# A decoder layer with experts on one core: result biases loaded into the self-attention's weights, padding written expert by expert, the main tiles' first row behind the early ones, opening loads in two steps, epsilon added by ScalarE

## The reference, cut to what matters

```python
x = layernorm(x + attn(x, x, x, sa_..., causal=True), ln1_g, ln1_b)
x = layernorm(x + attn(x, ctx, ctx, ca_..., causal=False), ln2_g, ln2_b)   # ctx: 4 x 1024 rows
# experts: 8 of them, each 256 -> 1024 -> 256; a row goes to its two best
topw, topi = top_k(softmax(xf @ router_w + router_b), 2); topw = softmax(topw)
h  = gelu(xf @ e_w1[e] + e_b1[e]);  eo = h @ e_w2[e] + e_b2[e]
x = layernorm(x + sum_e combine[:, e] * eo[e], ln3_g, ln3_b)
```

## Time and profile before

| | us |
|---|---|
| median of 3 executions | 1027.35 (1026.60 to 1029.22) |
| profiled execution, its own time | 1027.64 |
| span in the profile, first to last instruction | 1025.9 |
| TensorE busy | 969.8 (95%) |
| VectorE, ScalarE, GpSimd busy | 561.4, 583.2, 350.7 |

### The profile page before, as it was taken

How to read it: one execution, slowest core, us unless ns; L and a number is a source line. 1 busy time by engine, 2 the same in 40 slices (tenths; PEclk the granted TensorE clock), 3 DMA queues, 4 the chain that set the end, 5 groups by cost and what they waited for, 6 DMA issues and landing times.

```text
span 1025.9 us, 18784 instructions
## 1 busy us (share of the span) xinstructions
PE 969.8 (95%) x6052; PEld 578.2 (56%) x6053; DVE 561.4 (55%) x964; ACT 583.2 (57%) x1200; POOL 350.7 (34%) x469
## 2 busy tenths in 40 slices
PE   5999999999999999999999999984978999999995
PEld 3545544343445543435443354234977999999974
DVE  3746587877766777777778777622221121121216
ACT  2464556777765677775677657881322444343442
POOL 8465952343144443314554150112140111111114
PEclk9999999999999999999999999997988999999998
DMA  7533452003024011204333030012021243224116
GB/s 220 142 109 100 107 133 82 23 21 105 1 65 122 23 42 41 55 1 120 131 119 97 11 93 1 32 53 72 16 98 36 103 138 128 94 68 169 48 53 209
DMA packets 72001, 84.22 MB, mean 82 GB/s; under 512 B 10753, under 2 KB 65537, under 8 KB 71809
## 3 DMA queue, kind: packets, MB, share of 16 engines
q1 hardware_dynamic: 66432, 66.06, 22.2%
q0 software_dynamic: 5504, 17.34, 5.0%
HBM read 38.89 MB, written 12.63 MB: 50 GB/s over the span
## 4 chain that ended last, share of the span: by engine, by line
PE 86%; DMA 5%; DVE 2%; issue 1%; POOL 1%; SPq 1%; another core or an unknown queue 1%; ACT 1%; DVEq 0%; ACTq 0%; POOLq 0%
PE o_bank L867 15%; PE a_bank L850 15%; PE v_slot L1315 12%; PE v_slot L822 11%; PE a_bank L1307 9%; PE a_bank L790 6%; PE a_bank L805 4%; PE v_slot L826 3%; PE o_bank L1307 3%; PE v_slot L889 2%; DMA inputs<-slots_in 2%; PE v_slot L875 1%; PE v_slot L827 1%; PE a_bank L770 1%; DMA w_ca_wv<-in_ca_wv 1%
## 5 line engine op out<-in xcount | busy, mean ns | idle before, releaser
L1041 DVE TENSOR_REDUCE max_q<-v_slot 128x1 f32<-128x1024 f32 (+3 forms) x352 | 399.7, 1172 | 103.4 <-PE v_slot L822 65.7
L981 ACT ACTIVATE probs<-a_bank 128x512 f32<-128x512 f32 (+1 forms) x688 | 363.7, 589 | 111.6 <-PE a_bank L850 103.5
L1321 ACT ACTIVATE hidden<-a_bank,b 128x128 f32<-128x128 f32 x216 | 79.0, 367 | 171.2 <-PE a_bank L1307 149.1
L850 PE MATMUL a_bank<-q_stack_cross,k_stack_cross 99*128 99x512 bf16 x512 | 163.3, 381 | 0.7 <-ACT probs L981 0.5
L822 PE MATMUL v_slot<-k_stack_cross,q_stack_cross 96*128 96x512 bf16 x512 | 147.3, 379 | 0.0
L1315 PE MATMUL v_slot<-stack_or_weights,hidden 128*128 128x256 f32 x576 | 132.0, 383 | 14.0 <-DVEq L1157 13.9
L867 PE MATMUL o_bank<-probs,v_cross 128*32 128x512 f32 x1024 | 132.2, 603 | 0.1
L1315 PEld LDWEIGHTS v_slot<-stack_or_weights,hidden 128*128 128x128 f32 x576 | 107.7, 192 | 27.9 <-DVEq L1157 14.1
L1307 PE MATMUL a_bank<-x_col,stack_or_weights 128*128 128x128 f32 x864 | 113.0, 282 | 7.0 <-ACT hidden L1321 5.2
L1307 PEld LDWEIGHTS a_bank<-x_col,stack_or_weights 128*128 128x128 f32 x864 | 108.9, 198 | 9.6 <-ACT hidden L1321 5.4
L850 PEld LDWEIGHTS a_bank<-q_stack_cross,k_stack_cross 99*128 99x128 bf16 x512 | 44.3, 97 | 109.3 <-ACT probs L981 70.3
(11 more groups left out here) (209 smaller groups left out, 1142.5 us busy)
## 6 DMA issues: line engine op xcount, KB each, us to landing
stack_or_weights<-parts SPq DMA_DIRECT2D x96, 128.0 KB, 2.4
k_stack_cross<-parts SPq DMA_DIRECT2D x96, 128.0 KB, 2.4
stack_or_weights<-in_e_w SPq DMA_DIRECT2D x12, 1024.0 KB
q_stack_cross<-parts SPq DMA_DIRECT2D x48, 128.0 KB, 2.4
inputs<-in_ctxT POOLq DMA_DIRECT2D x4, 1024.0 KB, 6.6
stack_or_weights<-in_e_w SPq DMA_DIRECT2D x8, 512.0 KB
y_got<-token_out SPq DMA_DIRECT2D x16, 256.0 KB, 6.3
x_slots<-slots_in SPq DMA_DIRECT2D x30, 129.0 KB
```

The source lines that it names most:

```text
L850: last = nc.tensor.matmul(bank[:, i * cols:(i + 1) * cols], lhs, q_stack[kind][0:KM, G * u + j, q0:S], start=True, stop=True)
L981: nc.scalar.activation(probs[tile % PB][:, js[0]:js[-1] + 1, q0:S], a_bank[at % AS][:, 0:len(js) * (S - q0)].rearrange("p (j t) -> p j t", ...
L1041: nc.vector.tensor_reduce(most, rows, X, ALU.max, negate=True).then_inc(v_free, 1)
L1321: nc.scalar.activation(hidden[:, f, :], h_bank[f % HB][:, 0:P], ACT.Gelu, bias=b1[:, bass.ds(e * FC + f, 1)]).then_inc(flow.gelu_done, 1)
```

## The change

1. **Opening.** SyncE issues `sa_wq` and `sa_wk`, waits for `xT`, and then issues `ca_wv`, `ca_wk`, `sa_wv` and four bias columns. ScalarE itself issues the two bias columns it waits for. GpSimd loads `ctxT` after the constants and after `xT` has landed, and `x` behind its part of split 2. The memset of `k_stack_cross` goes; SyncE copies those rows from the other stack by two DMAs.
2. **Result biases.** The four weights of self-attention lie in one tile, and `b2` is that tile. SyncE loads it behind norm_turn of the last batch's self-attention.
3. **Last scatters.** "rank" issues four of the eight; the other four stand behind the result of the second expert's first tile. VectorE counts the tiles before it finishes that tile.
4. **Padding.** SyncE writes the padding of experts 0 and 1, and in the loop that of expert 2p+i+2 between its weights and its rows, and waits for it.
5. **Handover.** The two loads behind the early tiles' rows now bring main tile 0's rows, so that the last early tile transposes them; VectorE passes them on by increments, and TensorE's own transposition goes.
6. **End.** VectorE no longer adds epsilon; ScalarE does, into `fin_rstd`, and waits for it stand on ScalarE and GpSimd.

The diff, cut to its core:

```diff
@@ in_order
-    order = [("load_x", 0), ("load_ctx", 0), ("load_res", 0), ("constants",), ("more_constants",)]
+    order = [("load_x", 0), ("constants",), ("load_ctx", 0), ("more_constants",)]
...
-    for step, behind in ((("weights",), ...
+    for step, behind in ((("load_res", 0), ("split", 0, 2)), (("result_biases",), ("norm_turn", B - 1, 0)), (("weights",), ...
@@ decoder_layer
+        self_weights = sb("self_weights", [P, 4 * DC, D])
+        b2 = self_weights
...
-        b2 = sb("b2", [P, E, D])
@@ attention_sync
-                for n in ("sa_bq", "sa_bk"):
-                    sp.dma_start(bias[n][:, :], ...).then_inc(bias_in, 16)
+            sp.wait_ge(xt_in, 16)
+            for n in ("ca_wv", "ca_wk"):
+                sp.dma_start(w[n][:, :, :], ...).then_inc(cross_in, 16)
             sp.dma_start(w["sa_wv"][:, :, :], ...).then_inc(wv_in, 16)
-            for n in ("ca_wk", "ca_wv"):
...
+                elif k == "result_biases":
+                    sp.wait_ge(v_free, NO.v["out", B - 1, 0] + 1)
+                    sp.dma_start(b2[:, :, :], ...).then_inc(moe_const, 16)
...
             for e in range(EARLY):
-                end = expert_tiles(sp, early, e, lambda g, i: load_tile(sp, early, g, e * CAP + i * P))
-            for k in range(2):
-                load_tile(sp, early, ...end + k..., 0)
-            sp.wait_ge(v_free, NO.v["o_turn", len(UNIT_LIST) - 1] + 1)
-            sp.dma_start(b2[:, :, :], ...).then_inc(moe_const, 16)
+                expert_tiles(sp, early, e, lambda g, i: load_tile(sp, early, g, e * CAP + i * P))
@@ attention_gpsimd
                 elif k == "load_ctx":
+                    else:
+                        pool.wait_ge(xt_in, 16)
...
-                elif k == "more_constants":
-                    nc.gpsimd.memset(ones_rows(k_stack[1]), ONE_PAIR).then_inc(const_made, 1)
...
-                    early_part(pool, ev[1], lambda g: store_tile(early, g))
+                    if ev[1] < 2:
+                        early_part(pool, ev[1], lambda g: store_tile(early, g))
+                    else:
+                        store_tile(early, first_of_second(pool))
+                        scatter_late(2)
+                        scatter_late(3)
+                        early_part(pool, 3, lambda g: store_tile(early, g))
@@ attention_vector
-                        finish_tile(dve, early, 1, first_of_second(dve))
+                        second = first_of_second(dve)
+                        copy_column(dve, early, second + 1)
                         count_tiles(dve)
+                        keep_results(dve, early, 1, second)
+                        copy_row(dve, early, second + 2)
@@ block.sync
-            for e in range(E):
-                end = sp.value_load(end_i[0:1, e:e + 1], ...)
-                sp.dma_start(slots_dram[bass.ds(end, P), :], pad_rows).then_inc(pads_out, 16)
-            sp.wait_ge(pads_out, 16 * E)
+            for e in range(2):
+                pad_all(e)
+            sp.wait_ge(pads_out, 32)
             sp.wait_ge(scattered_late, 16 * 2 * QT)
             sp.wait_ge(counts_ready, 1)
...
+            for k in range(2):
+                first = sp.value_load(from_i[0:1, 0:1], ...)
+                load_tile(sp, early, ...early_count(sp) + k..., first)
...
                     load_weights(sp, 2 * pair + i + 2, i)
+                    pad_all(2 * pair + i + 2)
+                    sp.wait_ge(pads_out, pair * 32 + 16 * (i + 3))
+                    sp.sem_inc(passed, 1)
                     load_all(2 * pair + i + 2)
@@ block.tensor
-            transpose_row(pe, main, 0)
@@ block.scalar
+            for n in range(TT // FT):
+                sc.wait_ge(var_ready, FT * (n + 1))
+                nc.scalar.activation(fin_rstd[:, cols], fin_mv[:, cols, 1], ACT.Identity, bias=eps[:, :]).then_inc(fin_eps, 1)
+                if n and n - 1 not in ON_VECTOR:
+                    scale_back(n - 1)
@@ block.vector
+            dve.wait_ge(early.xcol_ready, count + 1)
+            dve.sem_inc(main.row_ready, 1)
+            dve.sem_inc(main.t_full, 1)
+            dve.sem_inc(main.xcol_ready, 1)
             dve.wait_ge(early.row_ready, count + 2)
-            copy_row(dve, main, 0)
-            copy_column(dve, main, 0)
             copy_row(dve, main, 1)
...
-                nc.vector.tensor_scalar(fin_rstd[:, cols], fin_mv[:, cols, 1], EPS, None, ALU.add).then_inc(var_ready, 1)
```

63 lines of the change are left out of this document (40 added, 23 removed).

## The result

| | changed kernel | kernel before, timed beside it |
|---|---|---|
| median of 5 runs | 1023.23 us (1020.91 to 1024.27) | 1028.97 us (1026.60 to 1033.53) |
| ratio | 0.9946, 95% interval 0.9929 to 0.9964 | |
| profiled execution | 1023.70 us, span 1022.0, granted clock 0.982 | 1027.64 us, span 1025.9, granted clock 0.982 |

What follows compares the result with a forecast made beforehand. TensorE, busy 95% of the span, was taken as the bound, with time to gain at its waits, lower clock and both ends. Terms -1.4 - 11.3 - 0.9 - 4.0 - 2.0 + 6.3 - 0.2 = -13.5 gave 1013.9 us, range 1006.5 to 1019.5.

Steps and rivals of the forecast that it cites:

- Opening: From the start to the first maxima: they begin 1.4 us earlier, bounds 0 and -2.2.
- The step on `xT`: In the opening: `xT` lands at 6.8 us instead of 8.1, sharing the DMA engines with two weights only.
- that on `ctxT`: In the opening: `ctxT`, issued at about 6.9 us, takes 7.0 and lands at 13.9 against 14.5.
- Result biases: First result near 698 us: the wait for the biases' load goes, -11.3 us; the earlier load costs 0, at most +1.
- -0.9 of clock: Behind the first result's wait: the lower clock may come or not, so half of 1.7 us was taken.
- Scatters and padding: Stop at 754 us: four scatters at a time instead of eight shorten it, -4.0 us, bounds -7.1 and +5.
- Handover: Early to main tiles near 781 us: -2.0 us, of it -1.3 start and -0.7 clock; bounds 0 and -4.7.
- The sum's third of a clock loss: Behind the handover: a third of the 2.3 us lost to the lower clock is regained, -0.7 us.
- Padding in the loop: At expert 2: padding behind two weights delays its rows, one TensorE stop, +6.3 us, bounds 0 and +10.
- The rival by which the padding passes the weights: At expert 2: padding lands 2 us after issue, the +6.3 are gone, 1007.6 us; chance 13%.
- the prediction's reckoning from that figure: At expert 2: by the skill page's 2 us, padding is back at about 814.3 and the term is 0.
- End: Last pairs: VectorE loses a 0.33 us step but GpSimd's pace stays, -0.2 us, bounds -0.8 and +0.5.

Runs made afterwards that it cites:

- e4: Changed kernel with the padding of experts 2 to 7 written in one go behind expert 1's rows, none in the loop; 1010.8 us, ratio 0.9905.
- e5: The changed kernel as it is, timed again in another group; 1017.1 us, ratio 0.9954.
- e14: Changed kernel with only the result biases' load moved from before six stack copies to behind the row maxima; 1014.5 us, ratio 0.9949.
- e3: Changed kernel with the whole opening of the kernel before; 1012.0 us, ratio 0.9913.
- e6: Changed kernel with both the opening of the kernel before (e3) and the padding ahead of the loop (e4); 1007.5 us, ratio 0.9875.
- e13: Changed kernel with the residual's rows loaded behind the first maxima's parts and the second stack's ones written by VectorE; 1010.9 us, ratio 0.9903.
- e11: e9 with the residual's rows loaded behind the second split again, as in the changed kernel; 1006.6 us, ratio 0.9856.
- e9: e7 with the new opening, residual behind the first maxima's parts, ones by VectorE, no waits for `xT`; 1000.9 us, ratio 0.9801.
- e15: e10 with the second stack's ones copied by SyncE again, as in the changed kernel; 1005.5 us, ratio 0.9837.
- e7: e6 with the result biases' load moved from before six stack copies to behind the row maxima; 1003.1 us, ratio 0.9821.
- e8: e3 with the result biases loaded after the last batch's row loads again, as in the kernel before; 1019.0 us, ratio 0.9975.
- e12: e7 with the last batch's eight scatters in one place again; 1002.2 us, ratio 0.9824.
- e16: e10 with the old handover, VectorE's two copies and TensorE's transposition, again; 1007.7 us, ratio 0.9862.
- e18: e10 with epsilon added by VectorE again, as in the kernel before; 1002.1 us, ratio 0.9766, in another group than e10.
- e10: e9 with context and cross weights waiting until `xT` has landed, as in the changed kernel; 1001.5 us, ratio 0.9804.
- e1: Changed kernel with the residual's rows loaded behind the first maxima's parts; 1015.7 us, ratio 0.9939.

## Why the prediction was wrong, step by step

- **Opening, forecast -1.4, was +5.0 to +8.5** in the four profiles with exactly this opening (the changed kernel, e4, e5, e14); the medians put what it loses against the old one at 3 to 5 us (e3, e6 against e4, e13). The failing step reads: "`x` is issued between two splits where GpSimd has idle time." It looked at GpSimd and not at the DMA engines, whose busy share in the trace of before was 0.76 from 10 to 20 us and 0.74 from 20 to 25. e11 prices it at 5.8 us on top of e9. The second is a cost that the sum never had: SyncE's two copies of ones, counted neither in issue time (1.41 us) nor in the queue of the row maxima (e15: 1.5 us in its profile, at most 4 by its time). The step on `xT` held (7.12 for 6.8), that on `ctxT` in this profile (14.39 for 13.9), but the load took 6.2 to 10.8 us in the twelve profiles with the gate, which no bound of mine had. "Everything behind is a chain of TensorE and VectorE work, so it shifts as a whole" held: the lag is 8.5 us from 80 to 520.
- **Result biases, -11.3 with -0.9 of clock, were -14.3 at their place**, as the first result's wait and the lower clock both went. But this was wrong: "the six copies behind it on SyncE's queue share the DMA engines with it for about as long, which covers them if TensorE needs them no sooner; I cost it at 0, at most +1." TensorE needed them sooner: the stop is 1.48 to 2.80 us in the eight profiles with the load there, and e7 shows 4.4 us with the clock. The net of the term was 6.3 us (e8 against e3).
- **Scatters and padding, -4.0, were -3.7 in the profile after** and -7.7 in that of e5. The first is within the bounds, the second 0.6 past them. The reason was wrong: I costed the scatters by their number. e12 shows that eight in a row cost nothing with two paddings beside them. In the profile after a stop of 2.19 us remains, in e5 none.
- **Handover, -2.0, was -4.7 and -3.1** (e5); e16 has 3.8. TensorE idles 2.0 us (forecast 3.5) in all 18 profiles with the new handover. Behind it the clock stays up in nine of them, the changed kernel's among them, and falls in the other nine, e5's to 0.59 from 774 to 778 us; that is the 1.6 us between the two values. What decides it is open. The sum's third of a clock loss was a mean of two cases, and in this profile it was luck.
- **Padding in the loop, +6.3, was +7.0.** The mechanism, its place and its size held: landing at 810.25 after 7.51 us, rows at 814.8, one stop at expert 2, none later. The rival by which the padding passes the weights fell. The Trainium skill, "DMA: Bandwidth & Descriptors", "Anatomy of one DMA", gives its fixed cost of about 2 us for a DMA on GpSimd's path and counts nothing that stands ahead of it. This write, on SyncE's queue behind two loads of 1 MB each, took 7.51 us, so the prediction's reckoning from that figure, 814.3, does not hold here. A load with nothing ahead of it does take 2.16 us.
- **End, -0.2.** The row "rest and end" is -1.5, and every one of the 18 experiments has -0.5 to -1.8 there, e18 with VectorE's epsilon too (-1.0). So epsilon is not what makes it; the rest may be the one profile of before.

The misses of the rows are +9.9, +4.9, -2.1, +0.3, -2.7, +0.7 and -1.3, 9.6 us in the profile; by the medians the miss is 7.8 us. Two of the failed steps are of one kind, a load moved into a stretch whose DMA traffic was not read; the third, the copies of ones, was not counted at all.

What would have shown the miss in time was the view of the DMA issues over the stretch into which a load is moved, with what is due there.

The experiments point past both kernels: e9 and e10 (new opening with the residual behind the first maxima and the ones by VectorE, padding ahead of the loop, biases in the calm stretch, new handover) run at 1000.9 and 1001.5 us, 0.980 of the kernel before, 19 to 20 us faster in the same group. The gate and the split scatters can go.

## What to carry to other kernels

A load that is moved off a path lands on another one: before moving it, read what is in flight and what is due in the 6 us behind its new place, on all DMA engines and on the issuing engine's queue, and not only whether the issuer is idle. When several small waits stand in a row, undoing one shows nothing; undo all, then put one back into the mended kernel. And put a write whose completion someone awaits ahead of the large transfers of its queue, not behind them.

## What was not expected of the hardware

The granted clock can fall without a stop that the profile shows. In the profile after, windows 500 to 525 and 525 to 535 us, TensorE is busy throughout, and still:

```profile
500.00:525.00 25.00, 25.00 (x148) 10.56 (x146) 19.77 (x28) 17.64 (x35) 12.77 (x12) 1.00 0.33 110
525.00:535.00 10.00, 10.00 (x60) 4.12 (x58) 5.42 (x10) 6.13 (x13) 8.05 (x7) 0.83 0.46 144
```

The number behind the five engines' busy times is the granted clock; the ends of matmuls are modelled, so gaps inside a busy stretch would not show. It cost 1.6 us, and the same instructions ran at the full level in the kernel before (516 to 527 us there, 1.00). e1, e5, e8, e11 and e15, late against it by 8.6, 5.0, 1.2, 6.8 and 4.2 us, lost 1.6 us at the same place, and the other 13 experiments, e14 with its 6.6 us of lag among them, did not. What decides it stays open. The 20 profiles differ in where they lose clock, and their mean clock goes from 0.982 to 0.997. Runs of one kernel differ too: by 11 us in ten runs of e4, by 8 in 31 of the kernel before and in four of e18.
